# Attention with ten probability slots, additions by accumulating transfers, and a new order of the work

## The reference

```python
qkv = x @ Wqkv                                  # 32 query heads of 32, one key head, one value head
scores = q @ k.T * 32**-0.5 + slope[h] * (pos_k - pos_q), masked where pos_k > pos_q
attn = softmax(scores) @ v
x = layernorm(x + attn @ Wo)
w = 4-bit group-wise quantized and dequantized ffn weight
x = layernorm(x + x @ w.T + bias)
```

## Time and profile before

| | |
|---|---|
| time, median of 3 runs | 2261.61 us (2260.55 to 2261.88) |
| profiled execution, its own time | 2261.66 us |
| its span (first to last instruction) | 2259.9 us, mean granted clock 0.996 |
| PE busy | 2214.5 us, 98% |
| VectorE busy | 1662.0 us, 74% |
| ScalarE busy | 999.0 us, 44% |
| GpSimd busy | 919.4 us, 41% |
| line 1155, values: PE | 307.1 us |
| line 242, maxima: PE, two largest groups | 152.3 and 152.2 us |
| line 1179, ones: PE | 130.0 us |

### The profile page before, as it was taken

The page is one execution under the profiler, slowest core; times in us unless marked ns, Lnnn a source line. Parts: engine busy times, 40 slices in busy tenths (PEclk is TensorE's granted clock), DMA queues, the critical chain, the costliest instruction groups (busy, mean ns, idle before and its releaser), DMA issues.

```text
span 2259.9 us, 36072 instructions
## 1 busy us (share of the span) xinstructions
PE 2214.5 (98%) x12303; PEld 1517.2 (67%) x12303; DVE 1662.0 (74%) x5002; ACT 999.0 (44%) x1950; POOL 919.4 (41%) x559
## 2 busy tenths in 40 slices
PE   7999999999999999999999999989999999999998
PEld 6888888655555555555555555537888888888887
DVE  6977778878888888888888888845656565656554
ACT  4222222167777777777777777770101010101010
POOL 0000000058878888887888887760101010101010
PEclk9999999999999999999999999999999999999999
DMA  6555554653442443343233223256333333333220
GB/s 232 190 182 194 202 186 141 178 126 89 110 100 77 114 110 82 95 114 99 56 95 91 73 76 96 58 174 179 91 95 91 93 92 91 94 89 97 87 80 28
DMA packets 179837, 257.02 MB, mean 114 GB/s; under 512 B 15446, under 2 KB 105686, under 8 KB 179306
## 3 DMA queue, kind: packets, MB, share of 16 engines
q1 hardware_dynamic: 179510, 254.87, 38.8%
q10 hardware_dynamic: 180, 0.33, 0.0%
HBM read 166.89 MB, written 87.20 MB: 112 GB/s over the span
## 4 chain that ended last, share of the span: by engine, by line
PE 70%; ACT 4%; DVE 3%; POOL 1%; issue 1%; SPq 1%; DMA 1%; ACTq 0%; POOLq 0%; DVEq 0%
PE pf L1418 30%; PE pa L1155 12%; PE pa L242 11%; PE pa L1139 11%; PE pa L1179 5%; ACT probs L1244 4%; DVE xm L261 2%; PE pf L1443 1%; POOL probs L1110 1%; DMA xk<-recip_d 1%; SPq L1317 0%; PE pa L251 0%; POOL probs L1096 0%; DVE late L1284 0%; DVE yt_lo L1563 0%
## 5 line engine op out<-in xcount | busy, mean ns | idle before, releaser
L1244 ACT ACTIVATE probs<-pa,slope 128x512 f32<-128x512 f32 (+3 forms) x1536 | 773.0, 588 | 241.6 <-PE pa L1139 147.2
L261 DVE CUSTOM_DVE_ANT_0 xm<-pa,xm 128x128 bf16<-128x128 f32 (+1 forms) x1488 | 750.3, 554 | 133.2 <-PE pa L242 120.5
L1110 POOL TENSOR_TENSOR probs<-probs 128x1024 f32<-128x1024 f32 x252 | 686.9, 2726 | 105.3 <-PE pa L1155 84.6
L1515 POOL TENSOR_TENSOR yb<-y,xm 128x1024 f32<-128x1024 f32 x32 | 76.6, 2395 | 648.1 <-DVE z L1528 632.7
L1155 PE MATMUL pa<-probs,v 128*32 128x512 f32 (+3 forms) x3072 | 307.1, 495 | 2.9 <-POOL probs L1096 2.9
L1472 ACT ACTIVATE ln<-ln 128x1 f32<-128x1 f32 x64 | 13.0, 203 | 490.2 <-DVE ln L1548 490.2
L1096 POOL TENSOR_SCALAR_AFFINE_SELECT probs<-probs 128x512 f32<-128x512 f32 x256 | 159.3, 634 | 107.1 <-ACT probs L1244 107.1
L1418 PE MATMUL pf<-ff_lo,xk 128*128 128x512 f32 x512 | 199.7, 390 | 0.0
L1089 POOL MEMSET credit<- 128x1 f32 x4 | 0.2, 98 | 460.8 <-POOLq L350 460.8
L681 ACT ACTIVATE q_hi<-ps,qscale 128x512 fp32r<-128x512 f32 x64 | 43.9, 688 | 283.8 <-PE ps L568 265.4
L1418 PE MATMUL pf<-fo_hi,xk 128*128 128x512 f32 x512 | 164.7, 393 | 0.0
(11 more groups left out here) (159 smaller groups left out, 4267.1 us busy)
## 6 DMA issues: line engine op xcount, KB each, us to landing
xm<-in_L_attn_hidden_states SPq DMA_DIRECT2D x8, 2048.0 KB, 9.3
q_hi_d<-q_hi SPq DMA_DIRECT2D x64, 256.0 KB, 2.0
q_lo_d<-q_lo SPq DMA_DIRECT2D x64, 256.0 KB, 2.4
att_d<-att SPq DMA_DIRECT2D x64, 256.0 KB
xm<-in_L_attn_hidden_states SPq DMA_DIRECT2D x32, 512.0 KB, 3.8
out<-z SPq DMA_DIRECT2D x32, 512.0 KB, 2.6
q<-q_hi_d SPq DMA_DIRECT2D x62, 256.0 KB, 6.0
xq<-q_hi_d SPq DMA_DIRECT2D x44, 256.0 KB, 5.2
```

The lines of the kernel that those rows point to most:

```text
L261: nc.vector.tensor_tensor_reduce(out=unused[:, 0:keys], in0=bank[:, 0:keys], in1=sh.distance[:, d0:d0 + keys], scale=1.0, scalar=-3e38, op ...
L1110: nc.gpsimd.tensor_tensor(o, o, probs[:, source % PR, h0:h1, 0:N], ALU.add).then_inc(add_done, 1)
L1244: nc.scalar.activation(probs[:, n % PR, h, 0:N], sc_ps[sc_ring.bank[use]][:, at:at + N], ACT.Exp, scale=slope[:, bass.ds(g * HPG + h, 1)]) ...
L1515: nc.gpsimd.tensor_tensor(yb[:, :], y[:, u, :], bias[:, :], ALU.add).then_inc(yb_done, 1)
```

## The change

- There are ten slots: six in `probs` (`KEPT`), four in `more_probs` (`MORE`), which lies where `fo_lo` is later. In the last step only the first six are used, and `fo_lo` is loaded in that step, when the last readers of the other four are done.
- GpSimd's list becomes: add 11 into 10, 10 into 9, 9 into 8, 7 into 8, 3 into 2, 2 into 1; and three additions by an accumulating transfer issued by GpSimd (`send`): 4 into 5, 6 into 7, 5 into 7. The transfer 5 into 7 waits until the other two have landed. So a step has two ones products, O0 and O8. In the last two steps nothing is added into unit 8, and in the last step 5 and 6 are added into 4 by instructions, so O4, O7 and O9 to O11 are made where they are needed.
- ScalarE copies `out_ps` to `att`, but for the last of all.
- The 512 + 128 columns of the maxima of query block 4 become 320 + 320.
- PE's order is one list for all steps but the last (`STEADY`, where a plus sign is the next step and a minus sign the one before) and one for the last (`LAST`); so are GpSimd's (`POOL_STEADY`, `POOL_LAST`) and the places of ScalarE's copies, counted in exponentials.
- SP puts the maxima of half 0 before it stores the values and sums of the step before, not after.

```diff
-PIECES += [(1, h, qb, k0, min((qb + 1) * P - k0, CH)) for h in range(HPG) for qb in range(BPH, QB) for k0 in (0, CH)]
+HALVED = (BPH + 1) * P // 2
+PIECES += [(1, h, qb, k0, HALVED if qb == BPH else min((qb + 1) * P - k0, CH))
+           for h in range(HPG) for qb in range(BPH, QB) for k0 in (0, HALVED if qb == BPH else CH)]
...
-    pool_order = [
-        ("cut", 2), ("cut", 0), ("cut", 1), ("cut", 3),
-        ("add", 2, 1, 0, 4), ("add", 3, 1, 0, 4), ("add", 5, 4, 0, 4), ("add", 6, 4, 0, 4),
-        ("cut", 8), ("cut", 9), ("add", 7, 8, 2, 4), ("add", 7, 8, 0, 2),
-        ("cut", 11), ("add", 11, 9, 0, 4), ("cut", 10), ("add", 10, 9, 0, 4),
+    STEADY = (
+        "V8- M+ M+ S M+ M+ S M+ S M+ V10- M+ L S S M+ V9- S S M+ M+ M+ S S M+ M+ S M+ S V6- M+ M+ S S V11- M+ "
+        "M+ S M+ S S M+ M+ V0 M+ M+ S S M+ M+ V1 M+ M+ S S M+ M+ S M+ S T+ O8- V2 V3 M+ M+ M+ S S V4 S M+ M+ "
+        "S S M+ M+ V5 V7 S S M+ M+ M+ S S M+ O0 S M+ S M+ S M+ M+ S S M+ M+ S S M+"
+    ).split()
+    POOL_STEADY = [
+        (1, ("cut", 10)), (1, ("send", 5, 7)), (1, ("cut", 11)), (1, ("cut", 9)), (1, ("add", 11, 10)),
+        (0, ("cut", 0)), (1, ("add", 10, 9)), (0, ("cut", 1)), (1, ("add", 7, 8)), (1, ("add", 9, 8)),
+        (0, ("cut", 2)), (0, ("cut", 3)), (0, ("add", 3, 2)), (0, ("add", 2, 1)), (0, ("send", 4, 5)),
+        (0, ("send", 6, 7)), (0, ("cut", 8)),
     ]
+    ACT_STEADY = [(18, "attended", 1, 1), (26, "attended", 0, 0), (33, "sums", 1, 1), (48, "sums", 0, 0)]
+    ADD_SECOND_AT = 39
...
+    def left_out(x):
+        return x[0] != "cut" and x[-1] >= ITS - 2 and x[2] == BPH * HALF
...
+    def slot(t, n):
+        return (t * NU + n) % (KEPT + MORE) if t < ITS - 1 else ((ITS - 1) * NU % (KEPT + MORE) + n) % KEPT
...
+            def may_add(kind, source, to, t):
+                pool.wait_ge(pv_done, block_done["V", to, t])
+                whole_unit(pool, t, source)
+                steps_through(pool, writers.get((t, source), []))
+                into = writers[t, to]
+                steps_through(pool, into[:into.index((kind, source, to, t))])
...
+            def send(source, to, t):
+                may_add("send", source, to, t)
+                pool.dma_start(prob(t, to), prob(t, source), accum_op=ALU.add).then_inc(sent_added[source, to], 16)
...
-                if 2 <= t < 2 + 2 * KT:
-                    n, k = divmod(t - 2, KT)
-                    sp.dma_start(raw(seam.fo[n][:, k:k + 1, :]), wo_d[n, :, k:k + 1, :]).then_inc(seam.w3_in[n], 16)
+                if 2 <= t < 2 + KT:
+                    sp.dma_start(raw(seam.fo[0][:, t - 2:t - 1, :]), wo_d[0, :, t - 2:t - 1, :]).then_inc(seam.w3_in[0], 16)
...
                 if last:
+                    for s in range(KEPT, KEPT + MORE):
+                        unit_read(sp, *tenant[s])
+                        for k in (2 * (s - KEPT), 2 * (s - KEPT) + 1):
+                            sp.dma_start(raw(seam.fo[1][:, k:k + 1, :]), wo_d[1, :, k:k + 1, :]).then_inc(seam.w3_in[1], 16)
                     half_of_third(sp)
```

More of the change, by code:

```diff
@@ L928, in attend @@
[L928 to L933, removed]
-    def pool_steps(t):
[L937 to L942, removed]
@@ L954, in attend @@
-    for t, x in add_list:
-        read_by_add[t, x[1]] = add_count[t, x]
-        added_to[t, x[2]] = add_count[t, x]
+    SENT = sorted({x[1:3] for t in range(ITS) for x in pool_steps(t) if x[0] == "send"})
+    readers, writers = {}, {}
+    for t in range(ITS):
+        for x in pool_steps(t):
+            if x[0] != "cut":
+                readers.setdefault((x[3], x[1]), []).append(x)
+                writers.setdefault((x[3], x[2]), []).append(x)
     EXPS = HPG * NU
@@ L961, in attend @@
         exps_through += [HPG * n + heads_at_once(unit) * (j + 1) for j in range(HPG // heads_at_once(unit))]
[L962 to L965, removed]
+    maxima, piece_at = [], {}
+    for t in range(ITS):
+        maxima.append([])
+        for kind, _, w in sequence(t):
             if kind == "M":
[L967 to L975, removed]
+                piece_at[w] = piece_at.get(w, -1) + 1
+            if kind in "MTL":
+                maxima[t].append((w, {"M": ("piece", piece_at.get(w)), "T": ("turn", 0), "L": ("turn", 1)}[kind]) if 0 < w < ITS else None)
+    mx_list = [(0, x) for x in FIRST] + [x for step in maxima for x in step if x]
     mx_use = {x: n for n, x in enumerate(mx_list)}
@@ L978, in attend @@
     sc_ring = Ring(SC, SCB)
-    PR = 6
     DIAG = [n for n, (c, i) in enumerate(units) if i >= BPH * c]
-    assert sorted(cuts) == DIAG
+    cut_list = [(x[2], x[1]) for t in range(ITS) for x in pool_steps(t) if x[0] == "cut"]
+    cut_count = {x: p + 1 for p, x in enumerate(cut_list)}
+    assert sorted(cut_list) == [(t, n) for t in range(ITS) for n in DIAG]
+    def slot(t, n):
+        return (t * NU + n) % (KEPT + MORE) if t < ITS - 1 else ((ITS - 1) * NU % (KEPT + MORE) + n) % KEPT
+    tenant, tenant_before = {}, {}
+    for t in range(ITS):
+        for n in range(NU):
+            tenant_before[t, n] = tenant.get(slot(t, n))
+            tenant[slot(t, n)] = (t, n)
+    assert all(slot(ITS - 1, n) < KEPT for n in range(NU))
     ctx = ExitStack()
@@ L1114, in body @@
                     if step[0] == "cut":
-                        cut(t, step[1])
+                        cut(*step[1:])
+                    elif step[0] == "add":
+                        add(*step[1:])
                     else:
-                        add(t, *step[1:])
+                        send(*step[1:])
             every_step(ITS, SLOTS, body)
@@ new lines, in body @@
+                to_score, to_max = iter(scores_order), iter(maxima[t])
+                for kind, n, s in sequence(t):
+                    if kind == "S":
+                        n, j = next(to_score)
+                        if j == 0 and n in (0, BPH):
+                            pe.wait_ge(neg_max[u][n // BPH], (i + 1) * PUTS)
+                        scores(t, u, n, j)
+                    elif kind == "V" and s >= 0:
+                        values(s, s % SLOTS, n)
+                    elif kind == "O" and s >= 0:
+                        total(s, n)
+                    elif kind in "MTL":
+                        found = next(to_max)
+                        if not found:
+                            continue
+                        w, item = found
+                        if item == ("piece", 0):
+                            pe.wait_ge(loaded[w % SLOTS], (w // SLOTS + 1) * LOADS if w > 1 else FIRST_HALF)
+                        if (w, item) == (1, ("piece", BPH * HPG)):
+                            pe.wait_ge(loaded[1], LOADS)
+                        maxima_item(w, w % SLOTS, item)
@@ L1224, in take_sums, with evacuate, between_exps @@
                 nc.scalar.copy(sums[:, c, :], sum_ps[:, :]).then_inc(sums_done, 1)
+            def evacuate(t, c):
+                act.wait_ge(pv_done, block_done["V", (BPH - 1, NU - 1)[c], t])
+                act.wait_ge(att_stored[c], t * 32 + CREDIT)
+                nc.scalar.copy(att[:, c, :], out_ps[:, :]).then_inc(att_done, 1)
+            def between_exps(t, at):
+                for where, kind, back, c in (ACT_LAST if t == ITS - 1 else ACT_STEADY):
+                    if where == at and t - back >= 0:
+                        if kind == "sums":
+                            take_sums(t - back, c)
+                        else:
+                            evacuate(t - back, c)
             def body(t, u, i):
```

156 lines of the change are left out of this document (75 added, 81 removed), and 12 rows, old and new, of the table plan.

## The result

The changed kernel takes 2452.82 us (median of 4 runs, 2442.48 to 2457.43) against 2261.08 of before: a ratio of 1.084, 95% interval 1.0824 to 1.0856. The forecast was 2216, its range ended at 2318, and the sign was wrong. The profiled execution, the fastest of the four, has a span of 2440.3 us, 180.4 more than before's.

What follows compares the result with a forecast made beforehand. TensorE bounds a step of 32.88 us now; after the change a circle through the transfers gives 31.3. 31 x (31.3 - 32.88) + 3 = -46 us from 2261.66 gives 2215.7; likeliest 2195 to 2240, range up to 2318.

Steps and rivals of the forecast that it cites:

- L: Time until transfers 4 to 5 and 6 to 7 have both landed; taken as 8.5 us, copies' range 6.7 to 9.3.
- the half-rate rival: GpSimd's wait before transfer 5 to 7: accumulating runs at half a copy's rate, step 34.4 to 36.5 us; chance 0.33.
- the prediction's circle: V3 to V5 on PE, both landings, transfer 5 to 7, GpSimd's list to cut 3: step at least 22.8 + L.
- the 22.8 taken: Step time besides L: 5.0 us of PE, 1.1 for issuing 5 to 7, 16.7 of GpSimd's cuts, additions and waits.
- The 2.43 us wait for O0 goes. Unit 6 comes next: Ten slots end ScalarE's 2.43 us wait per step; unit 6's exponentials then wait for O8, two thirds into the step.
- PE's 30.0: TensorE's work in one step after the change: 31.55 - 1.51 - 0.26 + 0.2 = 30.0 us.
- the sum: Whole kernel: 31 x (31.3 - 32.88) = -49, + 3 = -46 us, giving 2215.7 us.
- I leave it at 0 (plus or minus 3): Last step in its new order: no pieces, ScalarE sets its pace, so no change, plus or minus 3 us.
- GpSimd's issue: GpSimd's time to issue one accumulating transfer: taken as 1.0 us, bounds 0.3 and 4.8.
- the sign to look for: GpSimd idle 3 us or more before cut 11, with V9 or O8 waiting on GpSimd, would show half rate.
- The seam: Behind the last step, fo_lo's 4 MB load comes before xq and q2: +3 us, bounds 0 and 10.

## Why the prediction was wrong

**The step that failed is "I take 8.5" for L.** The mechanism was in the text, as the half-rate rival with its bounds of 11.6 to 13.7; the value taken was that of a copy. Measured, from the pair's first issue until both have landed, L is 13.5 us (12.6 to 14.7). For copies it is 8.6, so 8.5 was right for the wrong operation. My reason against the rival, that the pair has the queues to itself, was no argument: the pair alone fills them, at half the rate. The rows of copies could not rank the two ends, and I took their nearest as if they could. The sentence cited from the Trainium skill spoke for the upper end.

**A term was missing: the clock.** With L at 13.5 the prediction's circle gives 36.3 us; the step was 38.43. Of the 2.1 us between them 0.6 lie between the landing and the issue of 5 to 7, and 1.6 in the rest of the circle, 24.4 us for the 22.8 taken. A wait of 5 us in each step is followed by almost 4 us of work at about half clock; with TensorE kept busy the rest is 23.6 and the step 0.9 us shorter. The other 0.8 of the rest was not taken apart.

**"The 2.43 us wait for O0 goes. Unit 6 comes next"** was half right. ScalarE waits 1.9 us before unit 6 in every step, so only 0.5 us of it went, and with two transfers it waits 1.0 more for O5. The fastest step here with two ones products is 31.54, not PE's 30.0. In the sum this didn't show, since 31.3 came from the circle; that the copies' 31.57 lies so near it is in part luck, since the step doesn't follow L there.

**The last step, "I leave it at 0 (plus or minus 3)"**, costs more. From the addition of step 29 to the first product with Wo it is 18.0 us longer in the changed kernel (8.6 of them before the addition of step 30, which is still the circle's); with two transfers, free of the circle, it is 4.9 longer, and 1.7 shorter once the last step is reordered. The sum had no term for the start either, and the first addition comes 5.2 us later; why is open.

**What held.** The circle is there, with all its parts in their order. GpSimd's issue, 1.0 taken, is 0.877. The ones products are 71, within 69 to 72. The place of the wait, GpSimd before 5 to 7 with V9 behind it, and the sign to look for (3 us or more of idle time: 5.80) were right. The seam was taken at +3, and behind the first product with Wo it came out at -3: no wait for `fo_lo` shows there.

**GpSimd's order** wasn't a rival in the text. The transfers' half rate is worth some 220 us (2452.82 and 2229.89), and two changes of order alone are worth 77 and 152. With 5 to 7 issued later the kernel takes 77 us more; even with copies that order costs 6.7 us a step, 4.9 of them a wait for unit 5's slot. An addition put ahead of a transfer costs 152, by VectorE's addition.

## What to carry to other kernels

An addition by an accumulating transfer is cheap where nothing waits for it and dear in a chain: price it as two copies (1.94 here), and write down who waits for the landing, for the data and for the slot that it reads. Here the kernel with three transfers, of which one waited for the other two, was 192 us slower than the one before, and with two for which no step waited it was 9 faster. Where the trace has only a plain sister of the new operation, no row speaks for either end of the range, and the dearer end deserves at least an equal chance, above all where the price goes round a circle once in every step. A stall of TensorE can cost more than its length: here 4.8 us of it in each step cost 0.9 us more, through the clock of the work behind it.

## What the hardware showed

- An accumulating transfer of 1 MB within SBUF lands in 6.8 to 9.0 us (median 6.9) alone, and in 11.8 to 13.8 (12.5) when issued 0.9 us behind another; a copy in 4.5 to 6.7 (5.1) and 6.3 to 8.6 (7.7). With all queues full 197 to 239 GB/s move, counted once, and 383 with copies.
- To issue one costs GpSimd 0.877 us, and 0.547 as a copy (medians); 0.5 MB in place of 1 MB changes nothing (0.874 to 0.877).
- TensorE's granted clock fell to 0.50 (1.2 GHz) within an idle stretch of 5 us, from 1031.4 to 1036.2, and was back at 1.00 (2.4 GHz) in the stretch from 1040.
- VectorE's addition of two SBUF inputs (128 x 1536) took 5.20 us in place of 1.76 when it began 1 us after a GpSimd addition, and a GpSimd addition (128 x 2048) took 6.04 in place of 4.56 when it began 0.2 us after VectorE's: the later one ended when both, one after the other, would have.
